# Weighted edge values on the moving side of the aggregation, in high and low halves, for rounds 5 to 30

## The reference, cut to what matters

```python
Xq = (H @ W_lin.T).reshape(bt, n, h, dh)
Xv = (H @ W_val.T).reshape(bt, n, h, dh)
e = einsum('behd,hd->beh', leaky_relu(Xq[:, src] + Xq[:, dst], 0.2), a) + log(A0[src, dst] + EPS)
attn = softmax of e over the edges that share src
Vt = Xv[:, dst]
Y = segment_sum(attn[..., None] * Vt, src)     # for every node, the weighted values of its edges
return Y.reshape(bt, n, d) @ W_out.T
```

## Time and profile before

| | us |
|---|---|
| median of 3 runs (1185.16 to 1186.91) | 1185.27 |
| the profiled execution's own time | 1186.77 |
| its span in the trace | 1184.9 |
| TensorE matmul busy | 1155.7 (98%) |
| TensorE weight load busy | 1008.1 (85%) |
| VectorE busy | 992.8 (84%) |
| ScalarE busy | 813.3 (69%) |
| GpSimd busy | 388.5 (33%) |

### The profile page before, as it was taken

One profiled execution on the slowest core, in us unless ns is written; L12 is line 12 of the kernel. 1 busy time (PEld: TensorE's weight loads), 2 busy tenths in 40 slices (PEclk: granted clock), 3 DMA queues, 4 the chain that ended last, 5 costly groups with the idle time before them and its releaser, 6 DMA issues.

```text
span 1184.9 us, 23287 instructions
## 1 busy us (share of the span) xinstructions
PE 1155.7 (98%) x7564; PEld 1008.1 (85%) x7564; DVE 992.8 (84%) x2799; ACT 813.3 (69%) x1826; POOL 388.5 (33%) x710
## 2 busy tenths in 40 slices
PE   6999999999999999999999999999999999999998
PEld 5798898998988989989888788877777898889997
DVE  6998988888889888898888999988877789977664
ACT  4776886868868768588686766767777777753332
POOL 3130100100001001010011777766666477733332
PEclk9999999999999999999999999999999999999999
DMA  8220000000000000000000000000000000002222
GB/s 234 83 72 1 1 2 0 0 0 0 0 0 0 0 0 0 0 0 0 1 2 1 1 2 2 1 1 1 1 1 1 1 2 1 2 10 63 72 72 72
DMA packets 26319, 20.80 MB, mean 18 GB/s; under 512 B 1792, under 2 KB 22272, under 8 KB 26240
## 3 DMA queue, kind: packets, MB, share of 16 engines
q1 hardware_dynamic: 25664, 19.62, 5.8%
q10 hardware_dynamic: 576, 0.20, 0.1%
HBM read 11.42 MB, written 8.39 MB: 17 GB/s over the span
## 4 chain that ended last, share of the span: by engine, by line
PE 87%; DVE 8%; ACT 2%; issue 2%; DMA 1%; SPq 0%; DVEq 0%; ACTq 0%
PE ps L600 12%; PE ps L598 12%; PE ps L599 11%; PE ps L896 5%; PE ps L1507 5%; PE ps L1103 4%; PE ps L1515 2%; PE ps L660 2%; PE ps L646 2%; PE ps L912 2%; PE ps L882 2%; PE ps L666 2%; PE ps L672 2%; PE ps L1457 2%; PE ps L1092 2%; PE ps L1093 2%
## 5 line engine op out<-in xcount | busy, mean ns | idle before, releaser
L573 ACT ACTIVATE gate<-ps,b_lstm 128x256 f32<-128x256 f32 (+2 forms) x624 | 310.6, 565 | 96.4 <-PE ps L600 94.1
L598 PE MATMUL ps<-H_hi,w_hi 128*128 128x256 f32 (+2 forms) x624 | 210.5, 339 | 3.1 <-DVE srt L463 1.4
L599 PE MATMUL ps<-H_hi,w_lo 128*128 128x256 f32 (+2 forms) x624 | 205.1, 330 | 0.0
L600 PE MATMUL ps<-H_lo,w_hi 128*128 128x256 f32 (+2 forms) x624 | 192.6, 330 | 0.1
L131 POOL TENSOR_SCALAR rstd<-mv 128x8 f32<-128x8 f32 x16 | 5.2, 323 | 488.5 <-DVE mv L111 488.5
L598 PEld LDWEIGHTS ps<-H_hi,w_hi 128*128 128x128 f32 x624 | 117.4, 188 | 17.6 <-issue 4.0
L599 PEld LDWEIGHTS ps<-H_hi,w_lo 128*128 128x128 f32 x624 | 117.7, 189 | 8.1
L600 PEld LDWEIGHTS ps<-H_lo,w_hi 128*128 128x128 f32 x624 | 115.4, 189 | 10.5 <-DVE H_lo L527 2.0
L598 PE MATMUL ps<-hid_hi,w_hi 128*128 128x256 f32 (+2 forms) x384 | 120.3, 320 | 0.2
L599 PE MATMUL ps<-hid_hi,w_lo 128*128 128x256 f32 (+2 forms) x384 | 116.8, 311 | 0.0
L600 PE MATMUL ps<-hid_lo,w_hi 128*128 128x256 f32 (+2 forms) x384 | 106.3, 317 | 1.6 <-DVE hid_lo L527 1.0
(11 more groups left out here) (203 smaller groups left out, 3064.4 us busy)
## 6 DMA issues: line engine op xcount, KB each, us to landing
out<-x SPq DMA_DIRECT2D x32, 256.0 KB, 2.3
x<-in_x_in SPq DMA_DIRECT2D x4, 256.0 KB, 6.7
x<-in_WihT SPq DMA_DIRECT2D x1, 768.0 KB, 4.5
x<-in_WhhT SPq DMA_DIRECT2D x1, 768.0 KB, 6.7
x<-in_WihT SPq DMA_DIRECT2D x1, 256.0 KB, 8.1
x<-in_WqkvT SPq DMA_DIRECT2D x1, 192.0 KB, 4.1
w_sb<-in_W SPq DMA_DIRECT2D x1, 192.0 KB, 3.5
w_g<-in_Wg ACTq DMA_DIRECT2D x2, 64.0 KB, 4.1
```

The costliest lines, as they stand in the source:

```text
L573: nc.scalar.activation(gate[:, g, z, 0:w * GB], gate_bank(g, k, m)[:, 0:w * GB], ACT.Tanh if z == G else ACT.Sigmoid, bias=b_lstm[:, 4 * ( ...
L598: nc.tensor.matmul(dst, w_hi[:, src, p - 1, z], v_hi, start=start, stop=False)
L599: return nc.tensor.matmul(dst, w_lo[:, src, p - 1, z], v_hi, start=False, stop=False)
L600: return nc.tensor.matmul(dst, w_hi[:, src, p - 1, z], v_lo, start=False, stop=stop)
```

## The change

For rounds 5 to 30 (`turned(n)`) the sum per node is made the other way round: `hot_sT[c]` in fp32r is stationary and the weighted values move, 512 columns at once for all 4 graphs. Since fp32r holds fewer bits, the weighted values `va` are split first: ScalarE `high_part(n)` copies each chunk to `va_hi`; GpSimd subtracts for chunk 0 and VectorE (`low_part`) for chunk 1 into `va_lo`. So the sum takes 4 matmuls, but comes out with nodes on the partitions: ScalarE copies it (`copy_y`), TensorE transposes the 4 graphs into bank 4 (`features_first`), and ScalarE copies again (`copy_yT`) ahead of the projection. In rounds 0 to 4 and 31 `features_first` makes the straight sum as before, into bank 4. `va`, `yT` and the output bank are double now, `va_hi` and `va_lo` (in the memory of `xq_hi` and `xq_lo`) single, as are `y3` and `xv_hi`. `weigh` works on whole banks, 2 instructions of 128x512. TensorE's order in iteration n is `features_first(n-2)`, `values(n)`, `aggregate(n-1)`, `project(n-3)`, `softmax(NG + n)`. Elsewhere some pairs of semaphores are merged into one with counts doubled; the waits are for the same instructions (the attention's copy of `w_vo` now counts on `pool_made`).

```diff
-        hot_sT = sb("hot_sT", [P, EC, P])
+        hot_sT = sb("hot_sT", [P, EC, P], F32R)
...
-        va = hn[:, 0:EC * QB].rearrange("p (k b) c -> p k b c", k=EC)
-        y3 = hn[:, EC * QB:(EC + 1) * QB]
+        va = [hn[:, 0:EC * QB].rearrange("p (k b) c -> p k (b c)", k=EC), rl[:]]
+        y3, yT = hn[:, EC * QB:(EC + 1) * QB], [hn[:, (EC + 1) * QB:(EC + 2) * QB], hT3[:]]
+        va_hi, va_lo = (v[:].rearrange("p k b c -> p k (b c)") for v in (xq_hi, xq_lo))
...
+        def out_bank(n):
+            return ps[:, (3, 6)[n % 2]]
+        def turned(n):
+            return 5 <= n < NG - 1
+        def turned_to(n):
+            return sum(turned(m) for m in range(n + 1))
...
+            low_values(0)
+            for n in range(NG):
+                if n + 1 < NG:
+                    low_values(n + 1)
+                if turned(n):
+                    pool.wait_ge(SE["e_vh"], turned_to(n - 1) * EC + 1)
+                    if turned(n - 1):
+                        pool.wait_ge(SE["e_yp"], turned_to(n - 1))
+                    nc.gpsimd.tensor_tensor(va_lo[:, 0], va[n % 2][:, 0], va_hi[:, 0].bitcast(F32),
+                                            ALU.subtract).then_inc(SE["e_vl0"], 1)
...
             def weigh(n):
                 dve.wait_ge(SE["e_att"], n // PER + 1)
...
+                if n > 1 and turned(n - 2):
+                    dve.wait_ge(SE["e_vl0"], turned_to(n - 2))
+                    dve.wait_ge(SE["e_vl1"], turned_to(n - 2))
+                elif n > 1:
+                    dve.wait_ge(SE["e_yTp"], n - 1)
+                for c in range(EC):
+                    dve.wait_ge(SE["e_vp"], n * EC + c + 1)
+                    nc.vector.tensor_tensor(
+                        va[n % 2][:, c].rearrange("p (n d) -> p n d", d=DH),
+                        ps[:, c].rearrange("p (n d) -> p n d", d=DH),
+                        att[:, c, n * GH:(n + 1) * GH].unsqueeze(2).to_broadcast([P, GH, DH]),
+                        ALU.mult).then_inc(SE["e_va"], 1)
+
+            def low_part(n):
+                dve.wait_ge(SE["e_vh"], turned_to(n) * EC)
+                if turned(n - 1):
+                    dve.wait_ge(SE["e_yp"], turned_to(n - 1))
+                nc.vector.tensor_tensor(va_lo[:, 1], va[n % 2][:, 1], va_hi[:, 1].bitcast(F32),
+                                        ALU.subtract).then_inc(SE["e_vl1"], 1)
...
             for n in range(1, NG):
+                if turned(n - 1):
+                    low_part(n - 1)
                 weigh(n)
-                finish(n - 1)
-                softmax(NG + n - 1)
-            finish(NG - 1)
+                if n >= 4:
+                    finish(n - 4)
+                softmax(NG + n)
+            for n in range(NG - 4, NG):
+                finish(n)
...
             relu_part(NG - 2)
+            high_values(1)
             relu_part(NG - 1)
 
+            def high_part(n):
+                for c in range(EC):
+                    act.wait_ge(SE["e_va"], n * EC + c + 1)
+                    if turned(n - 1) and c == 0:
+                        act.wait_ge(SE["e_yp"], turned_to(n - 1))
+                    nc.scalar.activation(va_hi[:, c], va[n % 2][:, c], ACT.Copy).then_inc(SE["e_vh"], 1)
+
             def copy_y(n):
-                act.wait_ge(SE["e_yp"], n + 1)
-                if n > 0:
-                    act.wait_ge(SE["e_op"], n)
+                act.wait_ge(SE["e_yp"], turned_to(n))
+                if turned(n - 1):
+                    act.wait_ge(SE["e_yTp"], n)
                 nc.scalar.activation(y3, by4(ps[:, 2]), ACT.Copy).then_inc(SE["e_y"], 1)
 
+            def copy_yT(n):
+                act.wait_ge(SE["e_yTp"], n + 1)
+                if n > 1:
+                    act.wait_ge(SE["e_op"], n - 1)
+                nc.scalar.activation(yT[n % 2], by4(ps[:, 4]), ACT.Copy).then_inc(SE["e_yT"], 1)
+
+            for n in range(NG + 2):
+                if n >= 2:
+                    copy_yT(n - 2)
+                if 1 <= n < NG - 1:
+                    high_values(n + 1)
+                if n < NG and turned(n):
+                    high_part(n)
+                if n >= 1 and turned(n - 1):
+                    copy_y(n - 1)
+                if n < NG:
+                    exponentials(NG + n)
...
             def aggregate(n):
...
+                if turned(n - 1):
+                    pe.wait_ge(SE["e_y"], turned_to(n - 1))
+                for c in range(EC):
+                    pe.wait_ge(SE["e_vh"], turned_to(n - 1) * EC + c + 1)
+                    nc.tensor.matmul(ps[:, 2], hot_sT[:, c], va_hi[:, c], start=(c == 0), stop=False)
+                    pe.wait_ge(SE[("e_vl0", "e_vl1")[c]], turned_to(n))
+                    ins = nc.tensor.matmul(ps[:, 2], hot_sT[:, c], va_lo[:, c], start=False, stop=(c == EC - 1))
+                ins.then_inc(SE["e_yp"], 1)
+
+            def features_first(n):
+                pe.wait_ge(*((SE["e_yT"], n) if n > 0 else (SE["d_lr"], 2 * NG)))
+                if turned(n):
+                    pe.wait_ge(SE["e_y"], turned_to(n))
+                    for b in range(QB):
+                        ins = nc.tensor.transpose(ps[:, 4, b * T:(b + 1) * T], y3[:, b], ident[:])
+                else:
+                    pe.wait_ge(SE["e_va"], (n + 1) * EC)
+                    for b in range(QB):
+                        for c in range(EC):
+                            ins = nc.tensor.matmul(ps[:, 4, b * T:(b + 1) * T], va[n % 2][:, c, b * C:(b + 1) * C],
+                                                   hot_sT[:, c].bitcast(F32), start=(c == 0), stop=(c == EC - 1))
+                ins.then_inc(SE["e_yTp"], 1)
...
             values(0)
             gather(NG - 1)
-            for n in range(NG):
-                aggregate(n)
-                if n + 1 < NG:
-                    values(n + 1)
-                project(n)
-                if n == 0:
+            for n in range(1, NG + 3):
+                if 2 <= n < NG + 2:
+                    features_first(n - 2)
+                if n < NG:
+                    values(n)
+                if n == 1:
+                    softmax(NG)
                     for m in range(NG - BURST, NG):
                         logits(m)
-                softmax(NG + n)
+                if n <= NG and turned(n - 1):
+                    aggregate(n - 1)
+                if n >= 3:
+                    project(n - 3)
+                if n < NG:
+                    softmax(NG + n)
```

More of the change, by code:

```diff
@@ L1188, in edges_gpsimd, with low_values @@
                                             ALU.mult, ALU.add).then_inc(SE["d_hn"], 1)
-            for n in range(NG):
+            def low_values(n):
                 pool.wait_ge(SE["e_xvh"], n + 1)
@@ L1372, in edges_scalar @@
             relu_part(NG - 2)
+            high_values(1)
             relu_part(NG - 1)
+            def high_part(n):
[4 more added lines that the diff above has]
+                    nc.scalar.activation(va_hi[:, c], va[n % 2][:, c], ACT.Copy).then_inc(SE["e_vh"], 1)
             def copy_y(n):
-                act.wait_ge(SE["e_yp"], n + 1)
-                if n > 0:
-                    act.wait_ge(SE["e_op"], n)
+                act.wait_ge(SE["e_yp"], turned_to(n))
+                if turned(n - 1):
+                    act.wait_ge(SE["e_yTp"], n)
                 nc.scalar.activation(y3, by4(ps[:, 2]), ACT.Copy).then_inc(SE["e_y"], 1)
-            high_values(1)
-            for n in range(NG):
-                copy_y(n)
-                if n + 2 < NG:
-                    high_values(n + 2)
-                exponentials(NG + n)
+            def copy_yT(n):
[14 more added lines that the diff above has]
+                    exponentials(NG + n)
         def transpose(pe, n):
@@ L1500, in aggregate @@
             def aggregate(n):
-                if n > 0:
-                    pe.wait_ge(SE["e_y"], n)
-                for b in range(QB):
-                    if b % HB == 0:
-                        pe.wait_ge(SE["e_va"], (2 * n + b // HB + 1) * EC)
-                    for c in range(EC):
-                        ins = nc.tensor.matmul(ps[:, 2, b * T:(b + 1) * T], va[:, c, b], hot_sT[:, c],
-                                               start=(c == 0), stop=(c == EC - 1))
-                ins.then_inc(SE["e_yp"], 1)
@@ L1511, in project @@
-            def project(n):
-                pe.wait_ge(SE["e_y"], n + 1)
-                pe.wait_ge(*((SE["e_o"], n) if n > 0 else (SE["d_lr"], 2 * NG)))
-                for b in range(QB):
-                    ins = nc.tensor.matmul(ps[:, 3, b * C:(b + 1) * C], y3[:, b], w_out[:], start=True, stop=True)
+                if turned(n - 1):
[5 more added lines that the diff above has]
+                    ins = nc.tensor.matmul(ps[:, 2], hot_sT[:, c], va_lo[:, c], start=False, stop=(c == EC - 1))
@@ L1516, in project @@
+            def project(n):
+                pe.wait_ge(SE["e_yT"], n + 1)
+                if n > 1:
```

(4 more changed lines are left out.)

71 lines of the change are left out of this document (30 added, 41 removed).

## The result

The changed kernel takes 1198.74 us (median of 4 runs, 1197.48 to 1200.58) against 1185.22. It is slower by 13.5 us; forecast was 1200.0, 14.7 more. The profiled execution took 1197.6 with a span of 1195.6.

A forecast was written before the change was run, and what follows sets the result against it. TensorE's issue was taken to bound the pass; after the change a ring through ScalarE would. Entry to 1081.7, 24 rings (105.4) and a softmax total to 1187.5, tail 12.1: span 1199.6, median 1200.0 us, 8-in-10 range 1193 to 1210.

The forecast's parts named there:

- TensorE bounds the pass before, and its work falls.: Second pass: TensorE's issue sets 3.63 us per round; a turned round needs 3.27 of its work, 0.37 less.
- The ring: Turned rounds: transposes, values, sum, two high halves and copy_y form a closed loop of 4.39 us, against 3.63 before.
- 24 rings: From features_first(5) to features_first(29): 24 x 4.39 = 105.4 us, with 0.4 more for a softmax total.
- Entry: Second pass's start: values(1) at about 1058.45, 22.0 us of TensorE issue, features_first(5) loading at about 1081.7.
- the prediction's sign of being wrong: Turned rounds: a sum waiting for a low half would mean GpSimd or VectorE is in the ring.
- The 2.3: Second pass's start: the earlier values(1) gives back about 2.3 us.
- Tail: From the last ring to the span's end: last finish begins at 8.68, finish and store take 3.41, together 12.1 us.
- Sum: Whole kernel: span 1187.5 + 12.1 = 1199.6 us, 14.7 more than 1184.9; median 1200.0.
- VectorE's low half ... takes some 0.7.: Turned rounds: VectorE's low half begins at 3.85, takes some 0.7 us and is needed at 6.6.
- TensorE-bound: Rival: ScalarE's stretch between sum and transposes is 1.03 or less, ring 3.38, about 1176 us; chance 0.08.
- the rival with VectorE or GpSimd late: Rival: subtractions slow each other or a weighing falls behind, ring 0.2 to 0.4 longer, 1205 to 1210 us; chance 0.07.
- The clock: Rival: the ring's idle gaps halve TensorE's clock in stretches every second round, 20 us more, 1220; chance 0.05.

The follow-up runs named there:

- e8: e4 with copy_y placed between the two high halves on ScalarE: 1180.15 us, ratio 0.9948 to the kernel before.
- e1: Changed kernel with only ScalarE's queue reordered, copy_y(n-1) ahead of high_part(n): 1183.66 us, ratio 0.9986 to the kernel before.
- e10: Kernel before with only high_values(1) moved ahead of the first pass's last relu: 1182.96 us, ratio 0.9983 to the kernel before.
- e3: Changed kernel with no round turned, leaving only the longer pipeline: 1181.99 us, ratio 0.9977 to the kernel before.
- e6: Changed kernel without GpSimd's low half of chunk 0, its matmul rereading the high half: 1199.47 us, ratio 1.0121 to the kernel before.
- e5: Changed kernel with only every second round turned (1, 3, ... 29): 1181.58 us, ratio 0.9965 to the kernel before.
- e4: Changed kernel with transposes behind values(n) and, on ScalarE, high_values(n+1) ahead of copy_yT(n-2): 1180.43 us, ratio 0.9967 to the kernel before.
- e2: Changed kernel with an extra unused ScalarE copy between high halves and copy_y in rounds 6 to 30: 1210.45 us, ratio 1.0214 to the kernel before.

## Why the prediction was right

It held, in size and in mechanism; what was off inside it partly cancelled.

1. *TensorE bounds the pass before, and its work falls.* Right: a turned round's pieces are 3.19 in the chain of e8 (3.27 predicted) against 3.63, and e8 runs at 3.35. The 9.7 us of busy time are no measure of it: the page of e1, which has the changed kernel's instructions, gives 1154.2 and not 1146.0; a matmul that waits within the sum shows 0.50 there instead of 0.39, and its execution had the slow stretch.
2. *The ring.* Its pieces, from the transposes' first load at 1122.58: last values matmul 1.20 (predicted 1.29), last matmul of the sum 2.10 (2.23), first high half 2.59 (2.70), end of `copy_y` 4.23 (4.34), next load 4.34 (4.39). The ScalarE stretch is 1.64 (1.62 one round earlier), as summed from 0.63, 0.63, 0.60 and the overlap. The transposes were priced at 0.47 and took 0.39; the hand-over back was 0.12 (0.11 in the next round) instead of 0.05.
3. *24 rings.* From the load of `features_first(5)`, 1079.1, to that of `features_first(29)`, 1183.68, it is 104.6 us; 105.8 were predicted, with 0.4 for a softmax total that pokes out of the gap. Neither total did. One ring is 0.3 longer, the one from 1139.96 to 1144.61: there the first high half began 0.78 after the last matmul of the sum had started (1142.09 and 1142.87), and not 0.49. Why is not shown.
4. *Entry.* The values of round 1 load 3.36 after those of round 0 (predicted 3.37). The first transposes load 27.6 after `values(0)`, not 26.6. VectorE's maxima for the softmax took 1.39 beside GpSimd's subtraction (from 1074.65), so VectorE's low half for the first turned sum came late: the sum waited 0.15 for GpSimd's low half and then 0.57 for VectorE's, and the next weighing, late too, let the first high half begin 0.59 after the last matmul of the sum instead of 0.47. The term was missed by 1.0. So the prediction's sign of being wrong, a sum that waits for a low half, showed in this one round and not in the ring. The 2.3 that it gives to the earlier `values(1)` are not the work of the earlier high half alone: that is worth 1.0 (e10), and the whole longer pipeline 2.6 (e3).
5. *Tail.* 1195.6 - 1183.68 = 11.9 against 12.1. (The prediction's own terms 3.30, 0.05, 0.47 and 0.92 make 4.74 and not 4.77.)
6. *Sum.* 27.6 + 104.6 + 11.9 = 144.1 against the 144.5 that the prediction's span implies (1199.6 - 1055.1). This agreement is closer than its parts: rings 1.2 too long and an entry 1.0 too short cancel, and that is luck. The span itself, 1195.6, is 4.0 under the forecast, for the most part because this execution began its pass 3.6 earlier.
7. *"VectorE's low half ... takes some 0.7."* Wrong by 0.95: it took 1.65. It cost nothing there, since the ring left room (e6): it ended at 1123.68 and the sum loaded it at 1124.46. But the low halves are what the ring fell back on as soon as the first cause was removed (e1), and GpSimd's spoiled a part of e5.

The rivals: TensorE-bound needed ScalarE's stretch under 1.03; e1 and e4 show that the order decides it. Whether a second `va_hi` would do the same without a new order was not run. Of the rival with VectorE or GpSimd late the condition came true, since subtractions on both did slow each other, and its price did not: the ring is 4.34. The clock stayed at 1.00 through the whole turned stretch, with TensorE busy 82.95 of 105 us. The stretches of the changed kernel (PE, PEld, DVE, ACT, POOL busy, granted clock, DMA):

```profile
1079.00:1184.00 105.00, 82.95 (x501) 70.98 (x502) 86.03 (x103) 69.06 (x121) 60.56 (x49) 1.00 0.22 62
```

An idle gap of 1.1 us in every 4.3 did not bring the clock down in this kernel, and gaps of 1.5 did not in e2 (mean clock 1.0). The Trainium skill (page "TensorE: Matmul & The Clock Gate", section "A second HAM failure mode: psum-queue depth-cycling") describes another kernel whose clock swings between the two levels as TensorE idles briefly between groups of matmuls; the turned stretch idles as regularly and shows no such swing, at a clock of 1.00.

## What to carry to other kernels

When an edit lowers the bounding engine's work, follow each in-order queue once round the loop before counting the gain: here two helper copies written ahead of the one that TensorE waits for turned some 0.4 us of saved work per round into 0.7 us of loss. Reordering ScalarE's queue alone brought it back to the pace of the straight rounds (3.63 against 3.60); a gain over them came only with the transposes behind the values as well (3.44, then 3.35). A single buffer that a later round's producer waits for closes such a ring, and it costs where the waiting instruction stands ahead of a critical one in the same queue. When one ring is removed, price the next: after the swap it was the low halves, at 3.63; after e8 it was the values' own pair of buffers, at 3.35 and not TensorE's 3.19.

## What the runs showed of the hardware

VectorE and GpSimd, both subtracting two operands from SBUF, do not run side by side. In these timelines VectorE's 128x512 subtraction ends 0.54 to 0.55 after the one of GpSimd that it met, wherever it began. In the changed kernel GpSimd ran until 1123.13 and VectorE from 1122.02 to 1123.68 (1.66); in e8 GpSimd until 1123.52 and VectorE from 1123.20 to 1124.07 (0.87); in e1 GpSimd until 1131.23 and VectorE from 1130.40 to 1131.77 (1.37). Alone it takes 0.69 (e6). If VectorE's is under way first, GpSimd's takes 1.75 instead of 1.27 (e5); VectorE's took 0.83 there, since it met GpSimd's previous subtraction, which ended at 1150.20. VectorE's instructions with one operand in PSUM kept their times beside GpSimd: in e8 a pair of weighings took 1.28 from 1120.65, with GpSimd at work from 1120.87, and in the changed kernel the finish took 0.68 from 1120.72, wholly beside GpSimd's 1120.63 to 1121.91. The Trainium skill (page "SBUF — State Buffer", section "Who interferes with whom") states it as an exclusive lock on a port pair that the two engines share, taken by VectorE instructions with two SBUF inputs. The traces agree, with these numbers; the prediction did not price the new low half by it.
